# Attention scores as one fp16 product of 96 stacked rows per head

## The reference

```
x = x + tanh(g_xattn) * attention(layernorm(x), ctx, ctx)     # 16 heads of 32, 128 context rows per batch
x = x + tanh(g_ffn)   * ffn(layernorm(x))                     # shared network + 8 experts, top 2 of each token

att  = (q @ k^T) / sqrt(32)      # q = xn @ Wq^T + bq, k = ctx @ Wk^T + bk, each in heads
prob = softmax(att masked by pad_mask and subsq_mask)
out  = prob @ (ctx @ Wv^T + bv)
ffn  = sum over the top 2 experts of p_e * down_e(silu(gate_e(x)) * up_e(x)) + shared(x)
```

## Time and profile before

| | us |
|---|---|
| median of 3 runs | 1089.7 |
| lowest and highest | 1083.06, 1090.62 |
| the profiled execution | 1085.73 |
| its span, first to last instruction | 1083.5 |

### The profile page before, as it was taken

One profiled execution on the slowest core, in us unless ns is written; L12 is line 12 of the kernel. 1 busy time (PEld: TensorE's weight loads), 2 busy tenths in 40 slices (PEclk: granted clock), 3 DMA queues, 4 the chain that ended last, 5 costly groups with the idle time before them and its releaser, 6 DMA issues.

```text
span 1083.5 us, 31212 instructions
## 1 busy us (share of the span) xinstructions
PE 1012.0 (93%) x10160; PEld 778.7 (72%) x10161; DVE 775.1 (72%) x2795; ACT 500.1 (46%) x1010; POOL 425.3 (39%) x606
## 2 busy tenths in 40 slices
PE   5889899999999999999996599999999999989997
PEld 4678889888899888899984355555555555578885
DVE  4577888887898888888776566666666666545656
ACT  2456555456566566666542344444444444311111
POOL 4333355454555565554533222222212221045553
PEclk9787899999999999999998799999999999999999
DMA  9502565742455433236225243333333334169987
GB/s 369 222 21 90 211 135 100 111 103 73 54 103 109 109 100 89 60 81 184 89 82 135 68 128 117 116 115 113 113 114 116 116 116 145 60 182 329 303 292 262
DMA packets 76754, 147.30 MB, mean 136 GB/s; under 512 B 20912, under 2 KB 23088, under 8 KB 73872
## 3 DMA queue, kind: packets, MB, share of 16 engines
q1 hardware_dynamic: 46800, 68.11, 25.4%
q0 software_dynamic: 12896, 35.58, 11.3%
q10 hardware_dynamic: 16992, 42.74, 10.2%
HBM read 94.04 MB, written 52.35 MB: 135 GB/s over the span
## 4 chain that ended last, share of the span: by engine, by line
PE 75%; DVE 9%; issue 6%; ACT 4%; DMA 3%; POOL 2%; another core or an unknown queue 1%; SPq 0%; ACTq 0%; POOLq 0%; DVEq 0%
PE bank L1217 10%; PE bank L1225 9%; PE bank L1226 9%; PE bank L1227 9%; PE bank L1325 8%; PE bank L1301 5%; PE bank L1275 5%; PE bank L1277 4%; PE bank L1276 4%; PE bank L1285 2%; PE bank L1342 2%; PE bank L1340 2%; PE bank L1341 2%; DVE arena L887 2%; PE bank L1287 2%
## 5 line engine op out<-in xcount | busy, mean ns | idle before, releaser
L1275 PE MATMUL bank<-arena,weights 128*128 128x128 f16 x1024 | 185.3, 225 | 13.5 <-DVE arena L1018 8.7
L1277 PE MATMUL bank<-arena,weights 128*128 128x128 f16 x1024 | 185.1, 225 | 0.0
L1276 PE MATMUL bank<-arena,weights 128*128 128x128 f16 x1024 | 185.1, 225 | 0.0
L1217 PE MATMUL bank<-ident,arena 128*128 128x128 f32 (+1 forms) x1336 | 179.5, 270 | 2.5 <-DMA arena<-normed_rows,arena 1.9
L579 POOL DMA_INDIRECT arena<-normed_rows,arena x71 | 69.1, 973 | 250.1 <-PE bank L1217 225.0
L1217 PEld LDWEIGHTS bank<-ident,arena 128*128 128x128 f32 (+1 forms) x1336 | 143.8, 141 | 23.8 <-DMA arena<-normed_rows,arena 2.5
L527 POOL TENSOR_TENSOR arena<-arena 128x512 f32<-128x512 f32 x96 | 101.0, 1052 | 142.7 <-DVE arena L887 135.1
L1325 PE MATMUL bank<-arena 128*128 128x33 f32 x1024 | 137.3, 280 | 7.6 <-ACT arena L622 7.6
L1325 PEld LDWEIGHTS bank<-arena 128*128 128x128 f32 x1024 | 131.4, 200 | 14.7 <-ACT arena L622 12.2
L887 DVE CUSTOM_DVE_ANT_0 arena<-bank,arena 128x128 f32<-128x128 f32 x512 | 116.9, 284 | 31.2 <-PE bank L1301 31.2
L622 ACT ACTIVATE arena<-bank 128x512 f32<-128x512 f32 x128 | 75.9, 593 | 115.5 <-PE bank L1217 108.2
(11 more groups left out here) (196 smaller groups left out, 2268.9 us busy)
## 6 DMA issues: line engine op xcount, KB each, us to landing
expert_rows<-arena ACTq DMA_DIRECT2D x71, 256.0 KB, 2.2
arena<-in_x SPq DMA_DIRECT2D x64, 256.0 KB
x_rows<-arena SPq DMA_DIRECT2D x48, 256.0 KB, 5.4
arena<-x_rows SPq DMA_DIRECT2D x48, 256.0 KB, 3.8
weights<-in_w_gu ACTq DMA_DIRECT2D x8, 1024.0 KB, 7.0
normed_rows<-arena SPq DMA_DIRECT2D x32, 256.0 KB, 5.6
out<-weights ACTq DMA_DIRECT2D x32, 256.0 KB, 4.5
weights<-in_w_down ACTq DMA_DIRECT2D x4, 1024.0 KB, 13.5
```

The source lines that it names most:

```text
L1217: last = t.transpose(dst[:, c * P:(c + 1) * P], src[:, c * P:(c + 1) * P], (ident16 if src.dtype == F16 else ident)[:, :])
L1275: t.matmul(at, shared(c, part, 0, dc), x_hi_c, start=(c == 0), stop=False)
L1276: t.matmul(at, shared(c, part, 0, dc), x_lo_c, start=False, stop=False)
L1277: last = t.matmul(at, shared(c, part, 1, dc), x_hi_c, start=False, stop=(c == EC - 1))
```

## The change

The queries are no longer kept in fp32. Their bias comes from a matmul: a row of constants by `bq_half`, high and low half in rows 0 and 32 of a 64-row operand. ACT copies bank 0, scaled, to fp16 (`q_halves`, high half), and in the next iteration DVE writes the low half. SP stores both halves to DRAM, waits until they have landed, and loads them back as `q_stack`: rows 0 to 31 hold the high half, rows 32 to 63 the low half, rows 64 to 95 the high half again, four heads beside each other. The keys go the same way once, as high, high, low. One fp16 matmul of 96 rows then sums the three partial products of a head. The scores come out with a scale, which is put into the exponentials (`score_scale`). The lag of the scores and of all stages behind them grows by one. The score calls are (0), (1) together and (2), (3) together, one bank each. On SP, the x loads go ahead of the stores and the mask load to the end. Some tiles change places in the arena, some semaphores are merged, and the second chunk of down weights is loaded in iteration 34 instead of 32. The weights of queries and keys are no longer permuted on the host.

```diff
-        LQ, LS = 2, 3
+        LQ, LS = 2, 4
...
         def _(sp):
             def body(J, v):
+                n, j, u = tile(J, v, LQ + 1)
+                if live(n, NT):
+                    hold(sp, sp_passed, (q_ready, n + 1))
+                    sp.dma_start(q_dram[u].rearrange("a p n -> p a n"), q_halves.rearrange("p (a n) -> p a n", a=2)).then_inc(q_out[u], 16)
+                n, j, u = tile(J, v, 0)
+                if live(n, NT):
+                    need(sp, xn_ready, n - 1)
+                    sp.dma_start(x_in[u], x_tiles[bass.ds(j + u * HALF, 1)].rearrange("a p d -> (a p) d")).then_inc(x_here[u], 16)
+                n, j, u = tile(J, v, LX1 - 1)
+                if live(n, NT):
+                    need(sp, x1_ready, n - 1)
+                    sp.dma_start(x_res[u], x_tiles[bass.ds(j + u * HALF, 1)].rearrange("a p d -> (a p) d")).then_inc(res_here[u], 16)
                 n, j, u = tile(J, v, LX1 + 1)
                 if live(n, NT):
                     sp.wait_ge(x1_ready, n + 1)
                     sp.dma_start(x1_dram[bass.ds(j * P + u * S, P), :], x1[u]).then_inc(x1_out[u], 16)
+                n, j, u = tile(J, v, LQ + 1)
+                if live(n, NT):
+                    hold(sp, sp_passed, (q_out[u], 16 * (j + 1)))
+                    hold(sp, sp_passed, (s_done, group(n - 2, EC - 1)))
+                    stack(q_stack[u], q_dram[u], (0, 1, 0), q_stacked[u])
...
+                n, j, u = tile(J, v, LS - 3)
+                if live(n, NT) and u == 0:
+                    need(sp, sub_set, j)
+                    sp.dma_start(sub_raw, sub_tiles[bass.ds(j, 1)].rearrange("a p d -> (a p) d")).then_inc(sub_here, 16)
...
+            def stack(dst, src, parts, done):
+                for at, part in enumerate(parts):
+                    sp.dma_start(dst[at * D:(at + 1) * D, :].rearrange("d (h n) -> d h n", h=HG),
+                                 src[part].rearrange("(h d) n -> d h n", h=HG)).then_inc(done, 16)
...
             def beside(it):
+                if it == KEYS_IT:
+                    sp.wait_ge(k_lo_set, 1)
+                    sp.dma_start(k_dram.rearrange("a p n -> p a n"), k_halves.rearrange("p (a n) -> p a n", a=2)).then_inc(k_out, 16)
+                    sp.wait_ge(k_out, 16)
+                    stack(k_stack, k_dram, (0, 0, 1), k_stacked)
                 if it == NT:
                     sp.wait_ge(prep_lo, EXPERT_LO + EXPERT_CHUNKS)
                     load_down(0)
+                if it == NT + 2:
+                    sp.wait_ge(xt_done, NT)
                     load_down(1)
...
         def _(pool):
             def beside(it):
+                if it == 0:
+                    pool.wait_ge(scale_set, 1)
+                    g.tensor_scalar(bq_raw[:, :], bq_raw[:, :], w_scale[0:2 * D, 0:1], 1.0 / BIAS_PART, ALU.mult, ALU.mult).then_inc(bias_step, 1)
+                    pool.wait_ge(bias_step, 1)
+                    g.tensor_copy(bq_half[:, :], bq_raw[:, :]).then_inc(bias_step, 1)
+                    pool.wait_ge(bias_step, 2)
+                    g.tensor_tensor(bq_half[D:2 * D, :], bq_raw[D:2 * D, :], bq_half[D:2 * D, :], ALU.subtract).then_inc(bias_step, 1)
...
         def _(act):
-                        a.activation(sc, sc, ACT.Exp).then_inc(exp_done, 1)
+                        a.activation(sc, sc, ACT.Exp, scale=score_scale[:, :]).then_inc(exp_done, 1)
...
-                        last = a.activation(sc, sc, ACT.Exp, bias=peaks_neg[:, h - H + HG:h - H + HG + 1])
+                        last = a.activation(sc, sc, ACT.Exp, scale=score_scale[:, :], bias=peaks_neg[:, h - H + HG:h - H + HG + 1])
...
                     act.wait_ge(q_done, n + 1)
-                    need(act, s_done, group(n - 2, EC - 1))
-                    for c in range(EC):
-                        last = a.activation(q_t[u][:, c * P:(c + 1) * P], bank[0][:, c * P:(c + 1) * P], ACT.Identity,
-                                            scale=w_back[:, 0:1], bias=bq_s[:, c:c + 1])
-                    last.then_inc(q_ready, 1)
+                    hold(act, act_passed, (q_out[(v - LQ - 1) % 2], 16 * (j + u)))
+                    a.activation(q_halves[:, 0:E], bank[0][:, :], ACT.Copy, scale=Q_DOWN).then_inc(q_hi_ready, 1)
...
+                if it == KEYS_IT:
+                    act.wait_ge(scale_set, 3)
+                    a.activation(k_halves[:, 0:EC * B * T], k_full, ACT.Copy, scale=w_scale[:, 6:7]).then_inc(k_hi_set, 1)
...
         def _(dve):
+            link(d.memset(bq_top[:, :], 0.0))
+            dve.wait_ge(small_in, 96)
+            d.tensor_reduce(bq_top[0:2 * D, :], bq_raw[:, :], AX.X, ALU.max, apply_absolute_value=True)
             dve.wait_ge(wq_in, 16)
...
             def keys_and_values():
+                link(last)
+                d.tensor_reduce(peak[:, 20:21], k_full, AX.X, ALU.max, apply_absolute_value=True).then_inc(peak_set, 1)
+                top_peaks(2)
+                all_peaks(2)
+                scale_of(6, 20, SMALL_QK)
+                d.tensor_scalar(score_scale[:, :], w_back[:, 0:1], w_back[:, 6:7], 1.0 / Q_DOWN, ALU.mult, ALU.mult).then_inc(kv_set, 1)
+                dve.wait_ge(k_hi_set, 1)
+                d.scalar_tensor_tensor(k_halves[:, EC * B * T:], k_full, w_scale[:, 6:7], k_halves[:, 0:EC * B * T],
+                                       ALU.mult, ALU.subtract).then_inc(k_lo_set, 1)
...
                 normalise(1, LX1)
+                n, j, u = tile(J, v, LQ + 1)
+                if live(n, NT):
+                    dve.wait_ge(q_hi_ready, n + 1)
+                    d.scalar_tensor_tensor(q_halves[:, E:2 * E], bank[0][:, :], Q_DOWN, q_halves[:, 0:E], ALU.mult, ALU.subtract).then_inc(q_ready, 1)
...
         def _(pe):
                 def scores(k):
                     n, j, u = tile(J, v, LS)
                     if live(n, NT):
-                        pe.wait_ge(q_ready, n + 1)
-                        need(pe, max_done, group(n, k - 1))
-                        for c in range(EC):
-                            for g in (k, k + 1):
-                                rows = slice(g * D, (g + 1) * D)
-                                mm = t.matmul(bank[2 + g % 2][:, c * T:(c + 1) * T], q_t[u][rows, c * P:(c + 1) * P],
-                                              k_t[rows, c, u, :], start=True, stop=True)
+                        pe.wait_ge(q_stacked[u], 16 * PARTS * (j + 1))
+                        pe.wait_ge(k_stacked, 16 * PARTS)
+                        need(pe, max_done, group(n, k - 2))
+                        for h in range(HG):
+                            q_at, k_at = (h * EC + k) * P, ((h * EC + k) * B + u) * T
+                            last = t.matmul(bank[2 + k % 2][:, h * T:(h + 1) * T], q_stack[u][0:STACK, q_at:q_at + P],
+                                            k_stack[0:STACK, k_at:k_at + T], start=True, stop=True)
+                        last.then_inc(s_done, 1)
...
                         for co in chunks:
-                                last = t.matmul(dst, wq[:, 1, at:at + P], x_hi[:, xs], start=False, stop=(ci == EC - 1))
+                                t.matmul(dst, wq[:, 1, at:at + P], x_hi[:, xs], start=False, stop=False)
+                            last = t.matmul(dst, bq_half[:, co * P:(co + 1) * P], bias_row[:, :], start=False, stop=True)
...
                 turn_probs(0)
                 scores(0)
+                scores(1)
...
                 scores(2)
+                scores(3)
...
             def beside(it):
-                if it == 2:
-                    values()
+                if it == KEYS_IT:
+                    turn_peaks(2)
+                    values(0)
+                    spread_peaks(2)
+                    values(1)
```

More of the change, by code:

```diff
@@ L44, with build @@
 LO_UP = 2048.0
+SMALL_QK = 2.0 ** -20
+BIAS_PART = 32.0
+Q_DOWN = 2.0 ** -19
+STACK = 3 * D
+PARTS = 3
 EXPONENT = 0x7F800000
-def build(nc, x, ctx_t, pad, sub, gates, wq_t, wk_t, wv_t, bq, bk, bv, router, w_gu, w_down, s_gu, s_down, out):
+def build(nc, x, ctx_t, pad, sub, gates, wq_t, wk_t, wv_t, bq_rows, bk, bv, router, w_gu, w_down, s_gu, s_down, out):
     x_tiles = x.rearrange("b (j p) d -> (b j) p d", p=P)
@@ L157, in build @@
         x_hi, x_lo = carve(E // 2).bitcast(F16), carve(E // 2).bitcast(F16)
-        q_t = [carve(E) for _ in range(2)]
+        q_halves = carve(E).bitcast(F16)
+        q_stack = [carve(H * T // 2).bitcast(F16) for _ in range(2)]
         attn = carve(E)
@@ L190, in build, with by_expert, down_raw, down_halves @@
         tok_i = [carve(1).bitcast(I32) for _ in range(2 + LAST_LISTS)]
-        PLAN_AT = top[0]
+        top[0] = 0
+        down = carve(DOWN_END).bitcast(F16)
+        def by_expert(w):
+            return w.rearrange("p (x n) -> p x n", n=XD)
+        def down_raw(i):
+            if i == 0:
+                return slot(EXPERT_CHUNKS)
+            at = LATE_RAW_AT if i == 1 else (i + 1) * CH
+            return arena[:, at:at + CH]
+        def down_halves(i):
```

(17 more changed lines are left out.)

158 lines of the change are left out of this document (79 added, 79 removed).

## The result

The changed kernel is slower: 1100.45 us (median of 4 runs, 1097.83 to 1106.12) beside 1086.64 for the kernel before in the same comparison (1083.06 to 1090.62). The ratio is 1.0133, 95% interval 1.0069 to 1.0197. The forecast was 1081, faster. Its range held the time, its direction was wrong. The profiled execution took 1098.15 us with a span of 1096.1, against 1085.73 and 1083.5.

The account below looks back on a forecast made before the run. TensorE looked like the bound, the loop through VectorE, POOL and ScalarE close behind. Iterations 16 to 33 -12.6, 4 to 15 -8.4, extra iteration +11.5, start 8 - 8: total -9.5, forecast 1081 us, range 1060 to 1112.

Parts of the forecast that it names:

- Theory A: Whole kernel, from the follow-ups: the loss is the lag, the bias product and one-time work in the wrong place.
- theory B: Whole kernel, from the follow-ups: the loss is the stacks and their way through DRAM.
- The bias adds 4 products of 64 rows, 0.22 us.: Query products on TensorE: the added bias products cost 0.22 us a tile.
- 30.5 us pair: Rolled loop: a pair of iterations takes 30.5 us against 31.9, bound by the loop through VectorE and the chain.
- The rule on the drain: TensorE: a switch of tiling mode drains the engine; applied to the leaving scores, two gains of 0.09 us a tile.
- Start 8 - 8: Kernel start: lighter early iterations give back 8 us (0 to 11.5); bias and key stacking cost 8 (0 to 12).
- -8.4: Iterations 4 to 15: 0.7 us saved in each, -8.4 in all.
- the chain's 10.3 us: Loop, from VectorE's L1007 through POOL and ScalarE to the mix: forecast 10.2 us, down from 10.85.
- TensorE idle ahead of the even iteration's mix: Rolled loop, sign of being right: TensorE idle ahead of the even iteration's second mix, released by ScalarE.
- The round trip: Query halves through DRAM: 11.4 us from the iteration's start, scores due at 15.2 + 0.5; costed at nothing, cover 4.3.
- I leave that at nothing: Loop: moved stages swap parity against the expert splits; both VectorE steps cost alike, so costed at nothing.
- the 0.8 that the forecast gave to the new pass: POOL's norm (L556), 1.05 us: VectorE's new pass reads PSUM at that moment, so 0.8 us of the chain goes.

Follow-up runs that it names:

- the lag alone: Kernel before with scores one iteration later and the mask-row load moved behind the residual's load: ratio 1.0125; an earlier try without that load moved: 1.0967.
- the split moved along: Kernel before with scores and mask-row load one iteration later, and the split of the first down weights also one iteration later: ratio 1.0075.
- the three mendings: Changed kernel with bias product over 128 rows, first down-weight split one iteration later, two 1 MB expert loads at iteration 5: 1084.24 us, ratio 0.9967 to kernel before.

## Why the prediction was wrong

Theory A holds for most of the loss. With the runs' shares of the 1087 us: the lag +13.6 (8 the iteration itself, 5 the misplaced split), the score product -15.9, the 64-row bias +11.4 (1.0133 less 1.0028). Sum +9; measured +14. Each share is known to some 4 to 8 us, and nothing shows that they simply add up, so the 5 us that are left may be the stacks and their way through DRAM (theory B) or nothing; they were not isolated.

**The step that failed: "The bias adds 4 products of 64 rows, 0.22 us."** It measured 1.05 us a tile, and with 128 rows in the same place 0.23 (2.91 less 2.68). The mechanism of the loop was right: its 30.5 us pair is the 30.40 of the kernel with the bias over 128 rows. At its size it adds 0.87 us a pair (31.27 less 30.40), 13 us over 15 pairs, and the forecast would have been 1094, slower and within 1%. The rule on the drain stood two sentences further on, and was weighed only against what the change removes.

**"Start 8 - 8" failed.** Keys, queries and x loads queue on SP at the start and the stack then lands beside 2 MB of weights. The first 8, what the lag gives back, was 6.1 us at iteration 4 (the lag alone); the second 8, all that the change adds at the start, was 58.38 - 38.70 = 19.7, beyond its bound of 12. At iteration 16 stood +1.1 instead of -8.4. But moving the two loads took 7.1 us off at iteration 4 and nothing off the kernel, so what the late start costs in the end is open.

**The lag was priced too low.** The forecast had 11.5 - 8 = 3.5 us for it. Alone it costs 13.6, and 8 with the split moved along. The forecast counted what moves, and not the work that stays at a fixed iteration while the stages move past it.

**Right.** The 96-row product at 0.056. DVE's 14.8 and the chain's 10.3 us. TensorE idle ahead of the even iteration's mix, released by ACT (0.71). The round trip covered, 0.3 us of waits. The extra iteration, 12.3 for 11.5.

**Right in place, its cause not isolated.** POOL's norm at 0.27. DVE's timelines, of after and then of before:

```profile
445.05 0.68 DVE L977 SCALAR_TENSOR_TENSOR arena<-bank,arena 128x512 f16<-128x512 f32 x1
```

```profile
447.88 0.69 DVE L919 SCALAR_TENSOR_TENSOR arena<-arena 128x512 f16<-128x512 f16 x1
```

When the norm starts at 445.05, DVE is in the new pass (L977), as forecast. Before, the norm of 1.05 us started at 447.57, 0.14 us after DVE's L916, and ended at 448.62, when L919, which the forecast had not named, had just ended too (448.57). But the new pass is not needed for a shorter norm: with the lag alone the norm starts 0.14 us after the same L916 pass and takes 0.53, as DVE's next pass starts only at 430.02; and with the 64-row bias alone, without the lag or the pass, it takes 0.27 in both iterations. What the moved stages do to each other the forecast had dismissed ("I leave that at nothing"). With the lag alone it is worth 0.8 us a pair (31.09 in place of 31.9), so the 0.8 that the forecast gave to the new pass can't be credited to it alone.

## What to carry to other kernels

Read the row count of every product that is added, beside those around it: a small one of another row arrangement costs its neighbours, and zeros up to their rows are the cheaper form. When the lag of a pipeline grows, list what is tied to an iteration's number or parity (one-time work, loads shared by two tiles) and move it along. Price an idea alone first: here the product was worth 16 us and what came with it cost 30, of which 18 could be mended (1.0133 to 0.9967).

## What was not expected of the hardware

A 64-row fp16 product of 128 columns between 128-row ones costs 0.26 us of TensorE in all (0.10 ahead, 0.16 from its start), one of 128 rows 0.056. A 96-row product shows no such price: eight take 0.45 us, and the four transposes before them 0.47 us to the next start (435.13 to 435.60 in the changed kernel), as those before 128-row products do.

Three loads of 128 KB into 32 partitions each took up to 10.8 us (47.57 to 58.38) beside two loads of 1 MB, and 3.7 without them (to 51.25).

A wait of TensorE of 1.2 us a pair was followed by a lower granted clock in some pairs and not in others of one execution (0.71 behind 410.80, 1.00 behind 380.41, with the three mendings); waits of 0.7 us a pair in the changed kernel were not, from 280 to 500 us.
